# Six full jobs and nine mixed tiles in place of ten full jobs in each FFN layer

## The reference

```python
def ffn(role, x, W_down, b_down, W_up, b_up, gamma, beta):   # layers 0, 2, 3; 512 -> 256 -> 512
    h = einsum('bsh,bhk->bsk', x, W_down[role]) + b_down[role][:, None, :]
    h = gelu(h, approximate=False)
    y = x + einsum('bsk,bkh->bsh', h, W_up[role]) + b_up[role][:, None, :]
    yn = (y - mean(y)) * rsqrt(var(y) + 1e-5)
    return yn * gamma[role][:, None, :] + beta[role][:, None, :]

x = ffn(itok_B_1_2, x, ...)               # layer 0
x = core(x, lens, codes, ...)             # layer 1: attention, then cms and modifier MLPs, clipped to 0..1
x = ffn(itok_B_1_2, x, ...)               # layer 2
x = ffn(itok_B_1_2, x, ...)               # layer 3
```

## Time and profile before

| | us |
|---|---|
| median of three runs | 2485.66 (2485.14 to 2485.71) |
| the profiled execution | 2485.6 |
| its span | 2483.9 |
| TensorE busy | 2445.9 (98% of the span) |
| VectorE, ScalarE, GpSimd busy | 1022.2, 898.6, 402.7 |

### The profile page before, as it was taken

How to read it: one execution, slowest core, us unless ns; L and a number is a source line. 1 busy time by engine, 2 the same in 40 slices (tenths; PEclk the granted TensorE clock), 3 DMA queues, 4 the chain that set the end, 5 groups by cost and what they waited for, 6 DMA issues and landing times.

```text
span 2483.9 us, 27599 instructions
## 1 busy us (share of the span) xinstructions
PE 2445.9 (98%) x11362; PEld 2032.6 (82%) x11362; DVE 1022.2 (41%) x1415; ACT 898.6 (36%) x1227; POOL 402.7 (16%) x312
## 2 busy tenths in 40 slices
PE   8999999999999999999999999999999999999996
PEld 5878888888888888888888888888888888888885
DVE  4774334222333343223243332233433422268776
ACT  4664423222334332223243322232432222346653
POOL 2786000000000000000000000000100000028886
PEclk9999999999999999999999999999999999999998
DMA  7453111211111112111111111102111211144243
GB/s 260 179 206 110 68 51 51 85 51 40 46 68 51 51 51 85 36 49 51 68 52 51 47 72 51 51 32 87 51 35 51 85 51 43 59 162 145 77 145 136
DMA packets 41617, 195.32 MB, mean 79 GB/s; under 512 B 5762, under 2 KB 5762, under 8 KB 24852
## 3 DMA queue, kind: packets, MB, share of 16 engines
q1 hardware_dynamic: 35732, 151.60, 17.8%
q0 software_dynamic: 5760, 41.95, 4.2%
HBM read 162.07 MB, written 31.46 MB: 78 GB/s over the span
## 4 chain that ended last, share of the span: by engine, by line
PE 97%; DVE 1%; DMA 1%; POOL 0%; issue 0%; ACT 0%; DVEq 0%; SPq 0%; ACTq 0%; POOLq 0%
PE pair L57 23%; PE pair L59 23%; PE pair L58 23%; PE pair L963 2%; PE pair L971 2%; PE pair L970 2%; PE pair L962 2%; PE pair L961 2%; PE pair L969 2%; PE pair L454 2%; PE pair L456 2%; PE pair L455 2%; PE pair L420 2%; PE pair L938 1%; PE pair L922 1%; PE pair L452 1%
## 5 line engine op out<-in xcount | busy, mean ns | idle before, releaser
L1336 DVE TENSOR_TENSOR h_lo<-g,h_hi 128x512 fp32r<-128x512 f32 x256 | 178.9, 699 | 745.2 <-ACT h_hi L1160 744.9
L1158 ACT ACTIVATE g<-pair,bias_cols 128x512 f32<-128x512 f32 x256 | 176.6, 690 | 647.8 <-PE pair L59 411.5
L57 PE MATMUL pair<-h_hi,w_hiB 128*128 128x512 f32 x1024 | 399.0, 390 | 0.0
L59 PE MATMUL pair<-h_hi,w_loB 128*128 128x512 f32 x1024 | 398.4, 389 | 0.0
L58 PE MATMUL pair<-h_lo,w_hiB 128*128 128x512 f32 x1024 | 398.4, 389 | 0.0
L57 PE MATMUL pair<-o_hi,w_hiA 128*128 128x512 f32 x768 | 299.2, 390 | 0.0
L59 PE MATMUL pair<-o_hi,w_loA 128*128 128x512 f32 x768 | 298.8, 389 | 0.0
L58 PE MATMUL pair<-o_lo,w_hiA 128*128 128x512 f32 x768 | 298.7, 389 | 0.0
L1113 ACT ACTIVATE w_hiB<-w_raw 128x2048 fp32r<-128x2048 f32 x36 | 69.1, 1920 | 533.8 <-PE pair L59 504.9
L1548 POOL COPY acc<-xr 128x1024 f32<-128x1024 f32 x16 | 15.9, 1036 | 1358.1 <-PE pair L999 1349.8
L59 PEld LDWEIGHTS pair<-h_hi,w_loB 128*128 128x128 f32 x1024 | 192.2, 188 | 40.0
(11 more groups left out here) (236 smaller groups left out, 4371.6 us busy)
## 6 DMA issues: line engine op xcount, KB each, us to landing
w_raw<-in_units_a SPq DMA_DIRECT2D x32, 1024.0 KB
w_raw<-in_units_b SPq DMA_DIRECT2D x32, 1024.0 KB, 4.8
w_raw<-in_units_c SPq DMA_DIRECT2D x16, 1024.0 KB, 4.7
w_raw<-in_w_packed SPq DMA_DIRECT2D x30, 512.0 KB, 4.3
w_raw<-in_rows_packed SPq DMA_DIRECT2D x20, 512.0 KB, 4.6
x<-stage SPq DMA_DIRECT2D x32, 256.0 KB, 2.1
x_tok<-x SPq DMA_DIRECT2D x12, 512.0 KB, 7.5
first_gain<-in_rows_packed SPq DMA_DIRECT2D x10, 512.0 KB, 4.7
```

Source lines behind the costliest of these rows:

```text
L57: pe.matmul(out, lh, rh, start=(i == 0), stop=False)
L59: last = pe.matmul(out, ll, rh, start=False, stop=(i == len(terms) - 1))
L1158: act.activation(g[q % 2][:], bank[q % 4], ACT.Gelu, bias=bias_at).then_inc(gelu_done, 1)
L1336: v.tensor_tensor(h_lo[:, j, cols(n)], g[q % 2][:], h_hi[:, j, cols(n)].bitcast(F32), ALU.subtract).then_inc(hlo_done, 1)
```

## The change

Each FFN layer now has nine jobs in the order `KINDS`: O is a job of 8 sequences of one role as before, M a **mixed job** of three tiles (MT), each of two sequences of one role, whatever the roles of its neighbours. So a layer has 6 x 4 + 3 x 3 = 33 tiles. The routing table has 75 steps, and a row `role_row` of 15 roles for each layer (6 octets, 9 tiles).

```diff
+KINDS = "OOOMOMOOM"
+NP = len(KINDS)
+OCT = KINDS.count("O")
+MT = 3
+MIXED = MT * KINDS.count("M")
+NR = OCT + MIXED
+IN_OCT = OCT * GS
+JOBS = tuple((kind == "O", KINDS[:p].count(kind) * (1 if kind == "O" else MT)) for p, kind in enumerate(KINDS))
+T_OF = tuple(GT if octet else MT for octet, _ in JOBS)
+UNITS = tuple((at,) if octet else tuple(OCT + at + i for i in range(MT)) for octet, at in JOBS)
+TOKENS = NSEQ * LEN
...
+    def roles_of(self, eng, j):
+
+        octet, at = JOBS[j % NP]
+        layer = self.layers[j // NP]
+        low = ROLES * layer
+        found = [eng.value_load(self.routed.role_row[0:1, c:c + 1], min_val=low, max_val=low + ROLES - 1) - low
+                 for c in (layer * NR + unit for unit in UNITS[j % NP])]
+        return found * GT if octet else found
```

```diff
+    def pe_mix(self, pe, j, roles):
+
+        l = j // NP
+        pe.wait_ge(self.xlo_done, 2 * j + 2)
+        pe.wait_ge(self.wulo_done, ROLES * (2 * l + 2))
+        for t in range(MT):
+            ts = slice(t * P, (t + 1) * P)
+            to = self.turned[t // 2][:, t % 2, :]
+            w = self.wm[l][:, bass.ds(roles[t], 1)]
+            for k in range(KD):
+                hi, lo = w[:, :, k, 0:BN].rearrange("p a n -> p (a n)"), w[:, :, k, BN:2 * BN].rearrange("p a n -> p (a n)")
+                pe.matmul(to[:, 0:BN], self.xT_hi[:, k, ts], hi, start=(k == 0), stop=False)
+                pe.matmul(to[:, 0:BN], self.xT_hi[:, k, ts], lo, start=False, stop=False)
+                last = pe.matmul(to[:, 0:BN], self.xT_lo[:, k, ts], hi, start=False, stop=(k == KD - 1))
+            last.then_inc(self.mix_mm, 1)
+
+    def pe_back(self, pe, j, tiles):
+        for t in tiles:
+            if t == 0:
+                pe.wait_ge(self.hlo_done, KB * (j - 1) + KB)
+            pe.wait_ge(self.pre_done, self.MB[j] + t + 1)
+            for m in range(KB):
+                turn = pe.transpose(self.bank_D[m][:, t * P:(t + 1) * P], self.pre[:, t, m * P:(m + 1) * P], self.consts[4][:])
+                if t == MT - 1:
+                    turn.then_inc(self.down_done, 1)
+
+    def pe_job(self, pe, j, roles):
+
+        if self.octet[j]:
+            self.pe_down(pe, j)
+        else:
+            self.pe_mix(pe, j, self.roles_of(pe, j))
+            self.pe_back(pe, j, range(2))
+        if j:
+            self.pe_up(pe, j - 1, range(1), roles)
+        if not self.octet[j]:
+            self.pe_back(pe, j, range(2, MT))
...
+    def act_mixed(self, act, j):
+        for t in range(MT):
+            act.wait_ge(self.mix_mm, self.MB[j] + t + 1)
+            act.activation(self.pre[:, t, :], self.turned[t // 2][:, t % 2, 0:BN], ACT.Copy).then_inc(self.pre_done, 1)
...
-        act.activation(self.bank_D[m], self.bank_D[m], ACT.Gelu,
-                       bias=self.bias_down[:, bass.ds(role + ROLES * (j // NG), 1), m:m + 1].rearrange("p a b -> p (a b)"))\
-           .then_inc(self.gelu_done, 1)
+        for t, ts in enumerate(spans):
+            last = act.activation(self.bank_D[m][:, ts], self.bank_D[m][:, ts], ACT.Gelu,
+                                  bias=self.bias_down[:, bass.ds(roles[t] + ROLES * (j // NP), 1), m:m + 1].rearrange("p a b -> p (a b)"))
+        last.then_inc(self.gelu_done, 1)
```

```diff
+    def sp_load_down(self, sp, n):
+        j = self.job_of[n]
+        layer = self.layers[j // NP]
+        at = layer * NR + UNITS[j % NP][0]
+        if n >= self.SLOTS:
+            sp.wait_ge(self.down_done, KB * (self.job_of[n - self.SLOTS] + 1))
+        row = sp.value_load(self.routed.role_row[0:1, at:at + 1], min_val=0, max_val=3 * ROLES - 1)
+        sp.dma_start(self.wd_raw[n % self.SLOTS][:],
+                     self.w_packed[bass.ds(row, 1), :, 0:self.DOWN].rearrange("a p n -> (a p) n"))\
+          .then_inc(self.w_in[n % self.SLOTS], 16)
...
+    def sp_load_mixed(self, sp, l):
+        for r in range(ROLES):
+            sp.dma_start(self.wm[l][:, r, :, BN:2 * BN].bitcast(F32),
+                         self.w_packed[self.layers[l] * ROLES + r, :, 0:self.DOWN].rearrange("p (k n) -> p k n", k=KD))\
+              .then_inc(self.wm_in[l], 16)
...
-                for i in ((0, 1, 2, 3), (4,), (5, 6), (7,))[s]:
-                    sp.wait_ge(first.stored[i], 16 * STORES.count(i))
+                for i in ((0,), (1, 3), (5, 6), (2, 4, 7))[s]:
+                    sp.wait_ge(first.stored[i], first.stored_all(i))
```

## The result

The changed kernel takes 2494.81 us (median of 7 runs, 2493.80 to 2495.56); the kernel before took 2485.66 on the same chip (7 runs, 2483.74 to 2487.34). The ratio is 1.0037, with a 95% interval of 1.0026 to 1.0048: slower by 0.37%, where I had forecast 2468. The profiled executions stand at 2495.45 and 2485.6, their spans at 2493.7 and 2483.9: 9.8 apart.

A forecast was written before the change was run, and what follows sets the result against it. It took TensorE, with 97% of the chain, to bound the kernel. First layer with start -3, second and third layers -18.4, entry +2, tail -2.5 and lower clock +4 gave -18 on 2485.6: 2468 us, range 2434 to 2498.

The forecast's parts named there:

- first layer with start: First FFN layer, with lateness and the attention stage's beginning, plus the longer routing start (+2.9): -3 us together.
- entry to the last stage: Entry to the second and third FFN layers: third down load queued behind mixed loads and stores, +2 us (0 to +5).
- second and third layer: Second and third FFN layers: 2 x -11.4, plus 2 for weight work, plus 2.4 for GpSimd: -18.4 us.
- tail: End of the kernel, last job of three tiles: -2.5 us, bounds -4.5 and +1.
- lower clock, apart: TensorE dropping to its lower clock after two or three of the new gaps: +4 us, bounds 0 and 15.
- Rival D: 256-column matmuls don't start faster than 512-column ones, so at 0.227 the kernel is slower, 2503 us; chance 0.20.
- S+16.1: S is a mixed job's first mixed matmul; VectorE's last subtraction done 16.1 us later, leaving TensorE about 3.0 idle.
- Waits of a steady layer: Mixed-job waits 9.0 plus role loads 4.0, less 3.3 overlap: 9.7 us a layer, bounds 2 and 17.
- plus 2 for the work on mixed and up weights: Second and third layers: weight work falling between jobs 9 and 11 on ScalarE and VectorE, +2 us.
- A: The forecast itself: waits give back about half of the gain, 2468 us, range 2452 to 2480; chance 0.44.
- B: Pure sum: latencies hidden behind TensorE's transposes and up products, about -49 us, or 2437; chance 0.14.
- C: GpSimd bounds the first layer, 139 us instead of 135.6, giving 2480 us; chance 0.22.

The follow-up runs named there:

- mixed_order: Changed kernel; in mixed iterations ScalarE makes transposed copies before the norm and VectorE takes residuals earlier: 2486.53 us, ratio 1.0007.
- layer3_reuse: Changed kernel with the third layer using the second's up and mixed weights, its own neither loaded nor split: 2485.20 us, ratio 1.0004.
- entry_load: Changed kernel with the third down load back ahead of the mixed and gain loads at the entry to the last layers: 2488.38 us, ratio 1.0013.
- first_load: Changed kernel with the first layer's mixed weights issued before the down loads: 2488.87 us, ratio 1.0015.
- copies_first: Changed kernel with VectorE's residuals earlier in mixed iterations and ScalarE's transposed copies before the norm in every iteration: 2476.42 us, ratio 0.9964.
- all_tail: Changed kernel with five single edits combined, third-layer weights spread, splits ahead of statistics, GpSimd making the last two jobs' columns earlier: 2458.17 us, ratio 0.9890.

## Why the prediction was wrong

TensorE's unit prices held, and the stretches where loads, splits and the tail meet did not. Four steps of the sum failed, each named below: a load that it left out (6.1), the entry (4.6 over its term), the third layer's splits (6.6 over), and the tail (8.7 over). In the forecast's own terms the distance is 27.8 us (-18 to +9.8).

| term | forecast | measured |
|---|---|---|
| first layer with start | -3 | +7.1 |
| entry to the last stage | +2 | +6.6 |
| second and third layer | -18.4 | -10.0 |
| tail | -2.5 | +6.2 |
| lower clock, apart | +4 | in the rows above |

**Spacing: right.** 0.12 was taken from weight loads, 0.12 was measured. Rival D is out: 36 products with 37 loads fill 4.30 us. A window of the changed kernel (busy us and instructions of PE, PEld, DVE, ACT, POOL; clock):

```profile
117.90:122.20 4.30, 4.30 (x36) 4.30 (x37) 4.30 (x8) 0.97 (x3) 4.01 (x3) 1.00 0.02 4
```

This speaks against the literal reading of the Trainium skill ("TensorE: Matmul & The Clock Gate", The mechanism) that a load overlaps matmuls only where the row group differs: loads in a row are 0.12 apart, and so are these products with one full-array load each. Load and stream cannot stand one behind the other in that time. (For that reading I had 0.21 and 0.32; the rows' own 0.12 and 0.113 or 0.227 add up to 0.23 and 0.35. It changes nothing in the forecast.)

**The mixed job: right in size, half right in place.** 13.1 + 3.0 = 16.1 was forecast, and the five iterations that no weight or clock disturbs are 15.90 to 15.95. I had put the idle time ahead of the next down, and named residuals queued on VectorE as the reason for the upper bound. It was the residuals: 0.64 and 1.13 ahead of up products, 0.2 ahead of the down. The last low half, for which I had S+16.1, is done at S+14.9 (2416.92), so that the size agrees is in part luck. mixed_order shows the cause: with other orders on ScalarE and VectorE the same work takes 13.3.

**Waits of a steady layer: a little low.** 9.7 was forecast (2 to 17), 12.7 measured in layer3_reuse: 8.5 in mixed jobs (2.8 each), 4.2 in the octets around them. In the changed kernel itself the third layer, with its splits, has 21.4 (136.0 less 114.6), over the 17 that I had named as a sign of being wrong. The role loads were forecast at 4.0 before overlap and cost 2.7 to 3.2. The Trainium skill's floor of some 600 ns ("DMA: Bandwidth & Descriptors", Latency and other measured facts) did not show: 300 in the median on TensorE again.

**Second and third layer: the failing step is "plus 2 for the work on mixed and up weights".** It measured 8.6 in the three iterations that layer3_reuse shortens, and 9.8 by its span. I had asked whether VectorE has time on average, from a window of 40 us, and not what the splits stand ahead of in its order: 5.87 for three at 2337.29 delays the statistics and residuals behind them, and 4.26 at 2368.05 is waited for directly. I had also priced them as if GpSimd were idle, of which more below. This is 6.6 to 7.8 of the 27.8.

**Entry: the failing step is "+2 (0 to +5)".** It measured 6.6, above its bound. The queue that the load had been moved behind was named, but not the effect: ScalarE's split waits 10.83 for that load, and gelus are queued behind it. entry_load gives 5.7 of it back in the two iterations behind.

**First layer: the failing step is one that is missing.** The mixed weights' own load stands in no term of the sum. It is issued at 61.02, behind a wait of 16.33, and costs 6.1 by the span (first_load), 5.6 in job 2's iteration. Beside it, job 7's down waits 3.36, behind ScalarE's 2.99 for columns that GpSimd makes late (I had charged lateness to the gathers, and TensorE's transposes of gathered rows wait for none), and the attention stage's start costs a little more than the earlier trace rows: 2.07 for 1.47 at the query product.

**Start: right.** +2.9 was forecast (1 to 5.5), +3.9 measured in this execution, and +2.7 to +4.2 in the seven others with the same start.

**Tail: the failing step is its sign, -2.5 (-4.5 to +1).** It measured +6.2. "Each moving a third of a smaller job (-1.5)" gave 0.25: from the last scatter's issue to the end are 8.05 us, for 8.3 before. The two more scatters cost 2.55 (1.27 each, not 0.95). The other 3.9 came before the first of them: 0.8 until the last statistics, where the forecast had -1.1; 1.2 ahead of the first gain, where VectorE now loads roles; and 1.9 in gains and shifts, where it had -1.8. The last job's were indeed 1.2 cheaper, and the wait of 0.57 for the gain is gone, but the four operations beside GpSimd took 6.87 (3.45 + 3.42), for 3.89 before, and a second role load stands ahead of the last job's (0.66). No run tests these parts of the tail one by one.

**Clock: low.** Counting matmuls at twice their spacing, in us of extra time: 1.6 before, 9.0 after, so +7.4 where I took +4 (0 to 15). It lies inside the stretches above, and 1.45 of it, in job 3, is missing from the profiles of the other kernels. TensorE's busy sum fell by 40.6 and not by the forecast 55 to 63; the lower clock is 7.4 of that, and the rest was not traced.

**The rivals.** Against the -63 of TensorE's own work, A let waits give back two thirds; all of it and 9.8 more was given back. B and D are out. C did not bound the changed kernel, but for job 7's 3.36, and stood behind the other stalls: as soon as ScalarE's and VectorE's orders were mended (mixed_order, copies_first), GpSimd's columns paced the first layer, with 7.62 in one wait. Slower came by none of my rivals' mechanisms, but by four places that cost 6 to 9 us each, and that I had bounded too tightly or not listed.

**What stays open.** Whether GpSimd's share can be taken off the path where attention begins and in the tail. Two ways of giving part of it to VectorE brought 0.5 and 1.1 us, and why the tail grew to 54.8 in all_tail is read from its rows and not tested by a run of its own. Nor is it shown how much of copies_first is ScalarE's order and how much VectorE's.

## What to carry to other kernels

Where a change needs new operands, follow each one's load, split and first use through every queue it passes, and write a term for it; the average idle time of an engine says nothing about what stands behind an operation in its order. Where two halves of a job come complete together instead of one after the other, look first at whether each engine's written order serves the waited-for copy first: the new orders on ScalarE and VectorE together were 18.5 us here, and turned a loss into a gain. And when stalls are removed, expect the next engine to show at once: five single savings that sum to 44.3 us came to 25.6 in the first kernel that combined them. A part of that gap was that kernel's own: with its splits moved back, and the order of GpSimd's last steps changed, it was 37.1.

## What the runs showed of the hardware

VectorE's operations with two inputs in SBUF slow down beside GpSimd's. The same split of 128x1024 takes 1.21 us alone and up to 3.44 beside GpSimd's 128x1024 additions (the longest began at 2338.59, beside an addition that ended at 2340.94, and ended 1.08 after it). All of line 694 in the last stage, least, median and most in ns:

```profile
L694 DVE TENSOR_TENSOR last_wu_lo<-last_wu_lo,last_wu_hi x6: 1210/1214/3435, 2183.0 to 2341.9; 128x1024 fp32r<-128x1024 f32 x6
```

Of all splits of that shape in the changed kernel (L688, L694, L700), the eight that overlap GpSimd's gain or shift took 1.37 to 3.43 and the 28 others 1.19 to 1.23. The subtraction that reads PSUM (L714) stays at 1.21 to 1.23, in the 31 cases beside GpSimd's work as in the 14 without it. The Trainium skill ("SBUF — State Buffer", SBUF: two separate sides) says that a VectorE instruction with two SBUF inputs and a GpSimd one that reads SBUF share a pair of ports, which is locked for a whole instruction while the other engine waits. The durations agree, and that the reader of PSUM is spared agrees too.

A value load differs by engine: 300 ns in the median on TensorE, 277 on ScalarE, 290 on GpSimd, but 582 on VectorE (5 loads, 307 to 880). Scatters issued in sequence on GpSimd at the end stand 1.27 us apart, 0.97 of it the instruction and 0.30 between them.
